# Moving three normalisation stages, the output projection of attention and one preparation step into their neighbouring stages

## Time and profile before

| | us |
|---|---|
| median of 3 runs | 4138.01 (4137.37 to 4140.72) |
| the profiled execution's own time | 4135.73 |
| its span, first to last instruction | 4133.9 |
| PE, DVE, ACT, POOL busy | 4009.2, 3712.7, 2450.9, 1098.6 |

### The profile page before, as it was taken

The page is one execution under the profiler, slowest core; times in us unless marked ns, Lnnn a source line. Parts: engine busy times, 40 slices in busy tenths (PEclk is TensorE's granted clock), DMA queues, the critical chain, the costliest instruction groups (busy, mean ns, idle before and its releaser), DMA issues. The chain is left out here.

```text
span 4133.9 us, 108840 instructions
## 1 busy us (share of the span) xinstructions
PE 4009.2 (97%) x46275; PEld 2314.2 (56%) x46275; DVE 3712.7 (90%) x6341; ACT 2450.9 (59%) x2770; POOL 1098.6 (27%) x1156
## 2 busy tenths in 40 slices
PE   3999998999999999999999999999999999899999
PEld 2777775568764444444444444444444443677776
DVE  7999983689999999999999999999999995799998
ACT  1222225467777777777777777777777778122222
POOL 3888872300000000000000000000000000288886
PEclk8999999999999999999999999999999999999999
DMA  3000002310010110001001001001100110100000
GB/s 134 1 1 1 1 1 99 122 58 29 21 40 20 30 31 29 21 27 34 25 25 34 26 21 39 21 29 31 29 21 29 31 29 5 34 16 16 16 16 21
DMA packets 77709, 125.57 MB, mean 30 GB/s; under 512 B 27688, under 2 KB 56744, under 8 KB 75432
## 3 DMA queue, kind: packets, MB, share of 16 engines
q1 hardware_dynamic: 77224, 118.62, 9.8%
HBM read 72.55 MB, written 36.31 MB: 26 GB/s over the span
## 5 line engine op out<-in xcount | busy, mean ns | idle before, releaser
L971 DVE TENSOR_REDUCE stats<-ps_b 128x1 f32<-128x512 f32 x4016 | 2488.7, 682 | 105.7 <-PE ps_b L1020 6.3
L958 ACT ACTIVATE probs<-ps_s 128x1024 f32<-128x1024 f32 x2048 | 1983.8, 1021 | 649.6 <-PE ps_s L1054 649.6
L1020 PE MATMUL ps_b<-w_ffn 96*32 96x512 bf16 x10688 | 1112.0, 382 | 6.2 <-PEq L653 5.9
L1032 PE MATMUL ps_o<-probs,w_qkvT 128*32 128x512 f32 x8192 | 1090.5, 592 | 0.6 <-ACT probs L958 0.6
L1054 PE MATMUL ps_s<-w_ffn 99*32 99x512 bf16 x10752 | 977.0, 380 | 0.5 <-ACT probs L958 0.5
L545 PE MATMUL ps_gu_f<-w_ffn,zT_f 128*128 128x352 f32 x2048 | 634.9, 463 | 10.3 <-DVE h_f L450 9.4
L1054 PEld LDWEIGHTS ps_s<-w_ffn 99*32 99x32 bf16 x10752 | 365.7, 98 | 377.4 <-issue 188.8
L1020 PEld LDWEIGHTS ps_b<-w_ffn 96*32 96x32 bf16 x10688 | 357.7, 96 | 376.7 <-issue 174.0
L1020 PE MATMUL ps_b<-K,Q 96*32 96x512 bf16 x5376 | 558.6, 381 | 0.2
L1054 PE MATMUL ps_s<-Q,K 99*32 99x512 bf16 x5632 | 508.8, 381 | 2.2 <-ACT probs L958 1.8
L545 PEld LDWEIGHTS ps_gu_f<-w_ffn,zT_f 128*128 128x128 f32 x2048 | 383.1, 192 | 204.8 <-ACT zT_f L402 11.9
(11 more groups left out here) (124 smaller groups left out, 3084.9 us busy)
## 6 DMA issues: line engine op xcount, KB each, us to landing
qk_parts_dram<-qk_parts SPq DMA_DIRECT2D x96, 256.0 KB, 2.9
w_ffn<-qk_parts_dram SPq DMA_DIRECT2D x84, 192.0 KB
w_ffn<-qk_parts_dram SPq DMA_DIRECT2D x84, 128.0 KB
x_res<-in_L_attn_x SPq DMA_DIRECT2D x4, 2048.0 KB, 19.6
factor<-denom_dram SPq DMA_DIRECT2D x64, 128.0 KB, 5.3
out<-x_res SPq DMA_DIRECT2D x16, 512.0 KB, 2.6
v_then_heads<-OT SPq DMA_DIRECT2D x224, 32.0 KB
w_ffn<-qk_parts_dram SPq DMA_DIRECT2D x84, 64.0 KB
```

Of the source, the lines that this page charges most:

```text
L958: nc.scalar.activation(probs[:, (2 * kt + half) % 4, :], ps_s[:, half, :], ACT.Exp, scale=float(DH) ** -0.5).then_inc(exped, 1)
L971: nc.vector.tensor_reduce(mx[:, s, k // 4, bass.ds(k % 4, 1)], ps_b[:, bank, :], AX.X, ALU.max).then_inc(bank_free, 1)
L1020: last = nc.tensor.matmul(ps_b[j:j + STRIP, bank, :], Q[s][0:PAIRS, qt * P + j:qt * P + j + STRIP], K[s][0:PAIRS, kb * 512:(kb + 1) * 512] ...
L1032: last = nc.tensor.matmul(ps_o[32 * c:32 * c + 32, :], V[s][:, kt, :], probs[:, (2 * kt + c // 2) % 4, (c % 2) * 512:(c % 2 + 1) * 512], s ...
```

## The change

It has six parts.

1. The seven, one and six instructions of a norm become three methods of a class Norm that can be applied to a range of tiles (norm n1 is as before).
2. In f1, the statistics of tiles 0 to 47 are turned into rstd and shift inside the pipeline: DVE runs the variance part at the end of its step 54 and the finishing part at the end of step 56, ACT takes the square root at the end of step 55. At the end of its step 63, ACT normalises chunk 0 of the projection. The remaining 16 tiles are normed in the project block: variance first thing on DVE, root at ACT's step 2, the finish after DVE's third rest. Norm block n2 goes.
3. In the project block, PE turns chunk 1 after it has multiplied q and k of chunk 0, and ACT takes the high part of chunk 0 before it copies chunk 1.
4. Merge and f2 become one block. Merge has 6 PSUM banks in place of 8. DVE norms batch 0 after group 7, and does its feed-forward steps -3, -2 and -1 after groups 15, 18 and 21; PE turns tile 0 after group 21; the other 48 tiles are normed after group 31. PE's first gate and up product waits for all 32 residual adds and for the weights. Norm block n3 goes.
5. In both feed-forwards, the last tiles' PE order changes: the turn of a later tile's h comes before the down product of an earlier one.
6. Tiles move: z_quant and h_quant lie in the v tensor's free last part, hT of f2 in w_qkvT, the q and k parts in two tensors that attention uses later, OT and denom in y.

```diff
+class Norm:
+    VAR_STEPS, ALL_STEPS = 7, 12
+    def variance(self, dve, n, lo, hi):
+        nc, at = self.nc, slice(lo, hi)
+        mean, diff, var = self.mean[:, at], self.diff[:, at], self.var[:, at]
+        mean_e, m2_e, mean_o, m2_o = (self.m.stats[:, at, k] for k in (1, 2, 4, 5))
+        self.link(dve, nc.vector.tensor_tensor(mean, mean_e, mean_o, ALU.add), n, 1)
...
+        nc.vector.tensor_scalar(var, var, 1.0 / D, EPS, ALU.mult, ALU.add).then_inc(self.step, 1)
+    def roots(self, act, n, lo, hi):
+        act.wait_ge(self.step, n * self.ALL_STEPS + self.VAR_STEPS)
+        self.nc.scalar.activation(self.root[:, lo:hi], self.var[:, lo:hi], ACT.Sqrt).then_inc(self.rooted, 1)
+    def finish(self, dve, n, lo, hi):
+        dve.wait_ge(self.rooted, n + 1)
+        self.link(dve, nc.vector.reciprocal(rstd, self.root[:, at]), n, 8)
...
+class NormAhead:
+    LO, HI = 0, 3 * KT
+    AT = HI + 6
+    def vector(self, dve, i):
+        if i == self.AT:
+            dve.wait_ge(self.norm.stats_in, self.HI)
+            self.norm.variance(dve, 0, self.LO, self.HI)
+        if i == self.AT + 2:
+            self.norm.finish(dve, 0, self.LO, self.HI)
+    def scalar(self, act, i):
+        if i == self.AT + 1:
+            self.norm.roots(act, 0, self.LO, self.HI)
+        if i == NT - 1:
+            act.wait_ge(self.norm.done, 1)
+            normalise_chunk(self.nc, act, self.m, 0)
...
@@ ffn_phase, PE
                     if first:
                         turn_z(i, q, live)
+                    if i == NT - 1:
+                        turn_h(NT - LAG)
                     if live(-LAG):
+                        down(i - LAG)
...
+                for i in range(NT):
+                    at(step, i)
+                turn_h(NT - 2)
+                down(NT - 3)
+                down(NT - 2)
+                turn_h(NT - 1)
+                down(NT - 1)
@@ project_phase, PE
-                    if i + 1 < NC:
-                        pe.wait_ge(y_ready, i + 2)
+                    if i + 1 < NC and i != 0:
+                        turn_y(i + 1)
...
+                        if i == 0:
+                            turn_y(1)
+class Merge:
+    G = 2
+    NG = NT // G
+    PER_BATCH = NG // B
+    NORM_AFTER = PER_BATCH - 1
+    STEP_AFTER = {12: -4, 15: -3, 18: -2, 21: -1}
+    def bank(self, i):
+        return self.banks[(i + 4) % len(self.banks)].rearrange("p (t d) -> p t d", t=self.G)
+    def wait_weights(self, pe):
+        pe.wait_ge(self.w_loaded, 16)
+        pe.wait_ge(self.x_done, self.NG)
+    def gpsimd(self, pool, step):
+        scale_group(self.nc, pool, self.m, self.LASTG)
+        for i in range(-4, 0):
+            step(i)
+    def scalar(self, act, step):
+        self.norm.roots(act, 0, 0, KT)
+        for i in range(-4, 0):
+            step(i)
+        self.norm.roots(act, 1, KT, NT)
+    def vector(self, dve, step):
+        invert_denominators(nc, dve, m, self.LASTG)
+        for i in range(self.NG):
+            dve.wait_ge(self.y_done, i + 1)
+            nc.vector.tensor_tensor(tiles, self.bank(i), tiles, ALU.add).then_inc(self.x_done, 1)
+            dve.wait_ge(self.x_done, i + 1)
+            for t in range(G):
+                last = nc.vector.bn_stats(m.stats[:, i * G + t, :], m.x[:, i * G + t, :])
+            last.then_inc(self.norm.stats_in, 1)
+            if i == self.NORM_AFTER:
+                dve.wait_ge(self.norm.stats_in, i + 1)
+                self.norm.variance(dve, 0, 0, KT)
+                self.norm.finish(dve, 0, 0, KT)
+            if i in self.STEP_AFTER:
+                step(self.STEP_AFTER[i])
+        dve.wait_ge(self.norm.stats_in, self.NG)
+        self.norm.variance(dve, 1, KT, NT)
+        self.norm.finish(dve, 1, KT, NT)
```

More of the change, by code:

```diff
@@ L294, in norm_phase @@
 def norm_phase(nc, m, tag):
     with ExitStack() as ctx:
[L297 to L304, removed]
+        norm = Norm(nc, m, ctx, tag, m.va)
@@ L321, in _ @@
[L321 to L328, removed]
@@ L329, in _ @@
[L329 to L331 removed]
+                norm.variance(dve, 0, 0, NT)
+                norm.finish(dve, 0, 0, NT)
             @block.scalar
             def _(act):
[L335 to L336 removed]
@@ L341, in ffn_phase, with normalise_chunk @@
+def normalise_chunk(nc, act, m, i):
+    for j in range(CHUNK):
+        t = i * CHUNK + j
+        last = nc.scalar.activation(m.y[:, j, :], m.x[:, t, :], ACT.Identity, bias=m.shift[:, t:t + 1], scale=m.rstd[:, t:t + 1])
+    last.then_inc(m.y_ready, 1)
+def ffn_phase(nc, m, tag, out, lead=None, tail=None):
     with ExitStack() as ctx:
@@ L386, in halves, with at @@
             return ap.rearrange("p (a i) -> p a i", a=2)
-        def straight(step):
-            for i in range(-AHEAD, NT + LAG + 1):
-                step(i, i % 2, lambda k, i=i: 0 <= i + k < NT)
+        def at(step, i):
+            step(i, i % 2, lambda k: 0 <= i + k < NT)
+        if lead is not None:
+            lead.take_banks([ps_gu[:, c] for c in range(4)] + [ps_dn[:, c] for c in range(2)])
         with nc.Block() as block:
@@ L408, in step @@
                     if live(4):
+                        if lead is not None:
+                            lead.wait_norm(act, i + 4)
                         if live(2):
@@ L417, in step @@
                         nc.scalar.activation(halves(silu[:]), gate, ACT.Silu, scale=1.0 / SHRINK).then_inc(silu_done, 1)
-                straight(step)
+                if lead is None:
+                    for i in range(-AHEAD, 0):
+                        at(step, i)
+                else:
+                    lead.scalar(act, lambda i: at(step, i))
+                for i in range(NT + LAG + 1):
+                    at(step, i)
+                    if tail is not None:
+                        tail.scalar(act, i)
             @block.vector
@@ L484, in step @@
                         nc.vector.tensor_tensor(hs[:, q, :], hs[:, q, :], hM[:, q, :], ALU.add).then_inc(h_step, 1)
-                straight(step)
+                if lead is None:
+                    for i in range(-AHEAD, 0):
+                        at(step, i)
+                else:
+                    lead.vector(dve, lambda i: at(step, i))
+                for i in range(NT + LAG + 1):
+                    at(step, i)
+                    if tail is not None:
+                        tail.vector(dve, i)
             @block.gpsimd
@@ new lines, with __init__, take_banks, wait_norm @@
+    NORM_AFTER = PER_BATCH - 1
+    STEP_AFTER = {12: -4, 15: -3, 18: -2, 21: -1}
+    def __init__(self, nc, m, norm, ctx):
+        self.nc, self.m, self.norm = nc, m, norm
+        self.y_done, self.x_done, self.w_loaded = (ctx.enter_context(nc.semaphore(n)) for n in ("y_done", "x2_done", "ffn_w_back"))
+    def take_banks(self, banks):
+        self.banks = banks
+    def bank(self, i):
+        return self.banks[(i + 4) % len(self.banks)].rearrange("p (t d) -> p t d", t=self.G)
+    def wait_norm(self, act, tile):
+        act.wait_ge(self.norm.done, 1 if tile < KT else 2)
```

266 lines of the change are left out of this document (146 added, 120 removed).

## The result

The changed kernel takes 4125.12 us (median of 6 runs, 4121.84 to 4128.68), the kernel before beside it 4140.18 us (6 runs, 4137.37 to 4143.12): ratio 0.9964, 95% interval 0.9951 to 0.9977, some 15 us faster. On another chip, later, it was 0.9966 (0.9952 to 0.9979). Of the kernel before's runs beside the first experiments one took 8643.82 us and is left out of the ratios. The profiled execution took 4123.62 us with a span of 4121.8; the span before was 4133.9.

What follows compares the result with a forecast made beforehand. PE's busy share was distrusted; a DVE-POOL ring sets the feed-forward step, DVE merge's end. Gains 2.8 + 4.6 + 5.3 - 9.7 + 8.0 = 11.0 us took 4135.73 to 4124.7 profiled, median 4127.0, range 4116 to 4133.

Steps and rivals of the forecast that it cites:

- A: Last tiles of both feed-forwards: PE turns h early and stands ready; gain 1.3 us in f1, 1.5 in f2, 2.8 together.
- B: Seam from f1 to project: norm block n2 goes, one block boundary of 0.31 us stays; gain 4.6 us (4.4 to 4.7).
- C: Project's start to second q/k product: 15.6 us instead of 20.95, PE at full clock; gain 5.3 us (3.8 to 5.9).
- D: f1's steady state: 13 small DVE norm instructions held by POOL's; loss 9.7 us (bounds 0 and 13).
- E: Merge and f2 in one block: DVE sets the end, gate/up can start at 3574.2, not 3582.20; gain 8.0 us (3.2 to 9.5).
- F: Moved tiles and wider waits: same instructions, sizes and queues; zero, bounds of 1 us either way.
- near 5 and 2: f1 about steps 54 to 57: two pauses of PE near 5 and 2 us would show the hold on norm instructions.
- The part of a visit that I took as hidden: f1: DVE's idle 0.51 us and L467's held time of about 0.6 hide 1.1 us of each norm visit.
- cold either way: Merge into f2: PE rests some 4 us instead of 12 and is cold in both cases, so the following chain is as before.
- pieces not held: Rival in f1: the small instructions are not held and cost 1.2 us; gain 19.5, time 4118.5; chance 0.22.
- Merge bound by POOL or banks: Rival in merge: POOL's z steps 3.5 us apart, or PE short of banks; total gain 6 us, 4132; chance 0.13.
- PE staying at half clock: Rival in f1: after the 5 us pause PE is late every further step, some 8 us each; slower, 4151; chance 0.06.

Runs made afterwards that it cites:

- control: The changed kernel unedited, run again on another chip beside the kernels with one norm piece a step: 4124.13 us, ratio 0.9966 to the kernel before.
- tensor_tensor group: Kernel before plus eight groups of seven chained tensor_tensor on 48 columns in f1's DVE steps: ratio 1.0085, a group costs 4.5 us of 5.26.
- free reciprocal: Kernel before plus eight groups of seven chained reciprocals on 16 columns in f1's DVE steps: ratio 1.0022, a group costs 1.0 us of 1.97.
- tensor_scalar group: Kernel before plus eight groups of seven chained tensor_scalar on 48 columns in f1's DVE steps: ratio 1.0079, a group costs 4.5 us of 4.82.
- spread kernel: Changed kernel with the 13 norm instructions issued one a step (52 to 58, 60 to 65), chunk 0 in step 65: 4125.15 us, ratio 0.9965.
- late norm: Changed kernel with the norm of tiles 0 to 47 moved from DVE's steps 54 and 56 of f1 to 65 and 66: 4118.48 us, ratio 0.9954.

## Why the prediction was right

It was forecast that the kernel gains 11 us and that the profiled execution takes 4124.7; it gained 12.1 in the span and took 4123.62. The median was forecast at 4127.0 and came out at 4125.12; by the ratio the gain is 14.9 us, with an interval of 9.5 to 20.3 in which both 11 and 12.1 lie. By its own steps:

| part | forecast | measured |
|---|---|---|
| A, last tiles | +2.8 | +3.0 |
| B and C, norm block and first chunk | +9.9 | +10.5 |
| D, 13 instructions in the loop | -9.7 | -7.9 (-8.5 in the control) |
| E, merge into f2 | +8.0 | +8.3 |
| F and all else | 0 | -1.8 |

The sum is nearer than its parts by luck: part D cost 1.8 us less than forecast, and 1.8 us that the forecast had at nothing were lost elsewhere.

**A** was right in place and size, and undoing it alone gave 3.0 back in the two tails.

**B and C** came as said: 15.39 us from the last statistics to the second q/k product where 15.9 stood (15.6 and the block boundary of 0.31), the turn 1.06 where 1.04 stood. Their split was off. With C undone B alone gives 25.85 - 22.10 = 3.75, not 4.6, since a cold product took 8.49 us where it had been 7.64; C gives the rest, 6.7 where 5.3 stood.

**D** was the part on which the sign hung. The mechanism is shown: pieces held turn by turn with POOL's instructions, by kind and not by count. Even the sequence was as written: a piece until L570 (then L498) ends, one with L574, one with L579, one with L583, then free. PE paused 4.67 and 1.83 us where "near 5 and 2" stood. The size was 1.8 too high. The seven took 5.26 us, not 6.0, and the six 4.6, not 5.35: I had stacked each piece of 0.2 behind POOL's, but it ends with POOL's to within 0.1 us, and the finishing part's second instruction (0.25) was free. The Trainium skill, "SBUF — State Buffer", section "SBUF: two separate sides", had DVE's instructions in a two-port mode, or with two SBUF inputs (these only against a GpSimd instruction that reads SBUF), and GpSimd's lock each other out for whole instructions. The tensor_tensor group agrees (5.26 us). By this rule the held tensor_scalar (4.82), which has one input, would have to run in the two-port mode and the free reciprocal (1.97) not, which no run here shows outright. Two things in the traces fit it. A tensor_scalar on 704 columns takes 0.52 us, a tensor_tensor 0.89, so the first runs at another rate. And beside POOL's memset at project's start, which has no input, the norm's five two-input pieces on 16 columns took 0.14 to 0.19 us each, but its two tensor_scalars 1.51 and 0.96, both ending within 0.04 us of a memset's end.

The part of a visit that I took as hidden, 1.1 us, was a little low: 5.26 - 3.94 = 1.32 and 4.59 - 3.27 = 1.32 in the two visits, 1.3 in the first step behind a tensor_scalar group. With the restart of PE (0.65 in place of 0.5) and the shorter holds this makes 7.9 of the 9.7. It held in the spread kernel too (0.51 + 0.64). What failed there was the step of its expectation by which a piece costs no more than its own length: each of six pieces made L529 1.40 to 1.46 us longer.

**E**: 53.11 us from first add to product where 53.4 stood, the norm of batch 0 in 3.0 us where 3.3 stood, z steps of 2.25 where 2.27 stood, DVE the bound. What I had costed at nothing, "cold either way", moved by itself: after 4.16 us of rest the first product took 7.93 us, after 12 us it had taken 6.94, and in the control 6.66 after 3.94 us. It took 1.0 back in this trace. The clock granted from 3570 to 3574 us was the lower level:

```profile
3570.00:3574.00 4.00, 3.81 (x7) 0.50 0.00 0
```

**F and all else**: -1.2 us in f1's start-up and drain, +0.4 before f1, -1.5 in f2 besides A, of which 1.0 is that product, -0.4 in project and +0.9 in attend. Of the last two I make nothing: from the second q/k product to merge's first add nine kernels with the same code there took between 2871.2 and 2873.8 us. Of the 1.2 in f1, 0.8 lie before the second L548: 31.0 us from f1's start against 30.2, and the ten kernels with the same code there took 29.6 to 31.0 us. The rest, 0.36, is in the last two steps.

The rivals: with pieces not held (4118.5) the f1 steps would not have stretched, and the late norm shows by contrast what they cost. That its median is 4118.48, the number of this rival, is chance: it pays 2.9 us at the seam. Merge bound by POOL or banks (4132) fell with z steps of 2.25 us. PE staying at half clock (4151) fell: the product at 547.60 took 7.13 us after the pause, the next 4.90, so the clock came back within one product.

## What to carry to other kernels

Before you slip small VectorE instructions into a loop where GpSimd is busy, pair the starts and ends of the two engines: a tensor_tensor or tensor_scalar of 0.2 us (here f32 on 16 to 48 columns, no operand in PSUM) lasts as long as the GpSimd tensor_tensor beside it, and it can also push the loop's own small instructions behind a long one, so idle time in the loop does not pay for it. Put them where GpSimd is done (the drain), or use a kind that is not held. At a seam, ask for every wait whether it names the last event that is really needed: two adds fewer and no rest for TensorE were worth 3.2 to 5.5 us, more than the 2.4 by which the product came earlier.

## What I had not expected

- Almost the same rest before a product, very different prices. f2's first product took 7.93 us after 4.16 us of rest, 6.59 after 4.10, 6.66 after 3.94; 4.90 without rest. Its second, after 3.08 us of rest each time, took 6.66, 7.98, 6.66, 7.76 and 6.46. In f1 a product took 4.97 us after a rest of 1.83 and 6.66 after 1.99. The price is read from the clock granted during the product: 0.62 with 7.93 and 7.98 us, 0.74 with 6.66, 0.77 with 6.46, 1.00 with 4.90 and 4.97. Which rest makes the clock fall, and when it falls, I found no row to tell. It moves a single time by 1.5 to 3.1 us, so one trace does not settle a part of that size.
- GpSimd's memset holds some of VectorE's instructions and not others: the two-input pieces go free beside it, the tensor_scalars do not (the figures stand with part D above).
- A reciprocal, a reduce (0.42 us beside L595), and the product h, whose one input is in PSUM (0.83 us beside L600), are not held at all.
